# Node-wise programs between the edge passes of a four-layer graph network: six program phases per gap against one block, tile by tile

## The chip, the cores and the metric

The kernel runs on one core of a Trainium2 chip. The time is device microseconds (us) of one execution, median of three runs. TensorE does the matrix products, VectorE, ScalarE and GpSimd the element-wise work, and SyncE issues most DMAs. The profile records one execution.

## What is computed

3,125 nodes with 256 features each, 53,125 edges, all in float32. Four graph layers follow each other, each with a residual and a row norm around it. What lies between two edge passes works node by node:

```python
# end of layer 1 (8 heads)
out = jax.nn.elu(agg).reshape(n_nodes, h * c) + feat @ W_res
x = _layernorm(x + out)
# layer 2; what follows the first line stands in a loop of two, agg is the attention over the edges and the node itself
h = x @ w_in + b_in
xn = _layernorm(h, ln1_g[l], ln1_b[l])
q, k, v = xn @ wq[l] + bq[l], xn @ wk[l] + bk[l], xn @ wv[l] + bv[l]
...
h = h + agg @ wo[l] + bo[l]
xn2 = _layernorm(h, ln2_g[l], ln2_b[l])
h = h + gelu(xn2 @ w1[l] + b1[l]) @ w2[l] + b2[l]          # 256 -> 1024 -> 256
# behind the second of them
x = _layernorm(x + h)
all_h = einsum('ni,rio->nro', x, weight)                    # 8 relations: 256 -> 2048
```

The edge passes of layers 0 to 3, the sorting of the edges ahead of them and the last batch norm are the rest of the program.

## The kernel before

The nodes lie in 25 tiles of 128 (NT = 25), held in SBUF as one tensor `x` of 128 partitions by 25 by 256 (`h` inside layer 2 is the same tensor). The program is a row of phases. Each is a block with one instruction stream for each engine, and a block ends when all its engines are done; the next then allocates its buffers, loads its weights and starts. Three gaps lie between the edge passes. I call them A, B and C:

- A, behind the edge pass of layer 1 (`edge1`): `attend_update` (line 1794: divide by the head sums, ELU, add the residual projection, add to x, norm), `move` (line 2079: x to `x_rows` in HBM), `project` for w_in (line 1540 on), `Affine` (line 1868: statistics of the norm, and h saved to `h_rows`), `project` for q, k, v, whose output goes to `kv_rows`, from which the next edge pass gathers.
- B, behind the first attention pass (`edge2_0`): `self_merge` (line 2030: each node's own score and value merged with the edge sums, v and h loaded again from HBM), `project` for wo, `Affine`, `feed_forward` (line 1914), `Affine`, `project` for q, k, v.
- C, behind the second (`edge2_1`): `self_merge`, `project` for wo, `Affine`, `feed_forward`, `norm_into` (line 1845: x + h, norm), `project` for the 8 relations to `rel_rows`.

Inside `project` and `feed_forward` the work is already pipelined over tiles: ScalarE copies a tile (and applies the norm), TensorE turns it by two transposes (lines 1676, 1979), ScalarE or VectorE moves it out of PSUM, TensorE multiplies (lines 1666, 1990, 1972), VectorE or ScalarE takes the product out, SyncE stores it. `project` keeps 3 PSUM banks for turned tiles and 5 for products. `self_merge`, `attend_update`, `norm_into` and `Norm.statistics` (line 1745) work on whole 128 by 6400 tensors, or over all 25 tiles, on VectorE alone.

Of the kernel before, what the change touches and what calls it, by code (L numbers as in the profile page):

```python
# [1844 lines left out]
def norm_into(nc, tag, x, y, add=None, add_dram=None):  # L1845

    with Phase(nc, tag) as ph:
        norm = Norm(ph)
        own, loaded = ph.sem("own"), ph.sem("loaded")
        block = ph.block()  # L1850

        @block.sync
        def _(sp):
            sp.dma_start(add[:, :, :], node_rows(add_dram)).then_inc(loaded, 16)

        @block.scalar
        def _(act):
            norm.act(nc, act)

        @block.vector  # L1860
        def _(dve):
            step = Chain(dve, own)
            dve.wait_ge(loaded, 16)
            step(nc.vector.tensor_tensor(y[:, :, :], x[:, :, :], add[:, :, :], ALU.add))
            norm.dve(nc, dve, step, y, y)


class Affine:

    def __init__(self, nc, hold, tag, x, gain, bias, loads=()):
        self.scale, self.shift = hold.sb("row_scale", [P, NT]), hold.sb("row_shift", [P, NT])
        self.gain, self.bias = hold.sb("gain", [P, 2]), hold.sb("bias", [P, 2])
        with Phase(nc, tag) as ph:
            norm = Norm(ph)
            own, loaded = ph.sem("own"), ph.sem("loaded")
            block = ph.block()

            @block.sync  # L1880
            def _(sp):
                for dst, a in ((self.gain, gain), (self.bias, bias)):
                    sp.dma_start(dst[:, :], a.rearrange("(c p) -> p c", p=P), allow_slow_non_contiguous=True).then_inc(loaded, 16)
                for dst, a in loads:
                    sp.dma_start(dst, a, allow_slow_non_contiguous=True).then_inc(loaded, 16)
                sp.wait_ge(loaded, 32 + 16 * len(loads))

            @block.scalar
            def _(act):
                norm.act(nc, act)  # L1890

            @block.vector
            def _(dve):
                norm.scale_and_shift(nc, dve, Chain(dve, own), x, self.scale, self.shift)

    def copy(self, nc, out, x, t):

        return nc.scalar.activation(out, flat_tile(x, t), ACT.Identity, bias=self.shift[:, bass.ds(t, 1)],
                                    scale=self.scale[:, bass.ds(t, 1)])


class Dense:


    def __init__(self, ph, w1, b1, w2, b2):
        FF = w1.shape[1]
        self.w1, self.w2 = ph.sb("w1", [P, 2, FF]), ph.sb("w2", [P, FF // P, C])
        self.b1, self.b2 = ph.sb("b1", [P, FF // P]), ph.sb("b2", [P, C])
        self.loads = [(self.w1[:, :, :], w1.rearrange("(c p) f -> p c f", p=P)),
                      (self.w2[:, :, :], w2.rearrange("(f p) c -> p f c", p=P)),  # L1910
                      (self.b1[:, :], b1.rearrange("(f p) -> p f", p=P)), (self.b2[:, :], b2.partition_broadcast(P))]


def feed_forward(nc, k, tag, h, affine, dense):

    w1_s, w2_s, b1_s, b2_s = dense.w1, dense.w2, dense.b1, dense.b2
    FS = 4
    F = w2_s.shape[1]
    with Phase(nc, tag) as ph:
        copy = [ph.sb(f"copy{u}", [P, C]) for u in range(FS)]  # L1920
        turned = [ph.sb(f"turned{u}", [P, 2, P]) for u in range(FS)]
        inner = [ph.sb(f"inner{u}", [P, F, P]) for u in range(FS)]
        turn_p = [ph.ps(f"turn_p{n}", [P, 512]) for n in range(2)]
        up = [ph.ps(f"up{n}", [P, F // 2, P]) for n in range(4)]
        down = [ph.ps(f"down{n}", [P, 512]) for n in range(2)]
        copied, turn, moved, raised, bent, lowered, added, biased = (
            ph.sem(n) for n in ("copied", "turn", "moved", "raised", "bent", "lowered", "added", "biased"))
        block = ph.block()

        def tiles(eng, step):  # L1930

            def body(i):
                for u in range(FS):
                    step(i * FS + u, u)

            rounds(eng, NT // FS, body)
            for t in range(NT // FS * FS, NT):
                step(t, t % FS)

        def there(t):  # L1940
            return not isinstance(t, int) or 0 <= t < NT

        @block.scalar
        def _(act):
            def bend(t, u):
                after(act, lowered, t - FS + 1)
                for f in range(F):
                    act.wait_ge(raised, (2 * t + f // (F // 2) + 1))
                    last = nc.scalar.activation(inner[u][:, f, :], up[2 * (u % 2) + f // (F // 2)][:, f % (F // 2), :],
                                                ACT.Gelu, bias=b1_s[:, f:f + 1])  # L1950
                    if f % (F // 2) == F // 2 - 1:
                        last.then_inc(bent, 1)

            def fetch(t, u):
                after(act, turn, t - FS + 1)
                affine.copy(nc, copy[u][:, :], h, t).then_inc(copied, 1)

            def step(t, u):
                if there(t + 1):
                    fetch(t + 1, (u + 1) % FS)  # L1960
                bend(t, u)

            fetch(0, 0)
            tiles(act, step)

        @block.tensor
        def _(pe):
            def lower(t, u):
                pe.wait_ge(bent, 2 * t + 2)
                after(pe, added, t - 1)  # L1970
                for f in range(F):
                    last = nc.tensor.matmul(down[u % 2][:, 0:C], inner[u][:, f, :], w2_s[:, f, :], start=(f == 0), stop=(f == F - 1))
                last.then_inc(lowered, 1)

            def turn_tile(t, u):
                pe.wait_ge(copied, t + 1)
                after(pe, moved, t - 1)
                for c in range(2):
                    last = nc.tensor.transpose(turn_p[u % 2][:, c * P:(c + 1) * P], copy[u][:, c * P:(c + 1) * P], k.ident[:, :])
                last.then_inc(turn, 1)  # L1980

            def step(t, u):
                if there(t + 1):
                    turn_tile(t + 1, (u + 1) % FS)
                pe.wait_ge(moved, t + 1)
                for half in range(2):
                    after(pe, bent, (t - 2) * 2 + half + 1)
                    for f in range(half * F // 2, (half + 1) * F // 2):
# [12 lines left out]
        def _(dve):  # L2001
# [13 lines left out]
            def step(t, u):  # L2015
# [5 lines left out]
                if there(t - 2):  # L2021
                    add(t - 2, (u - 2) % FS)
# [317 lines left out]
```

## Time and profile before

| | us |
|---|---|
| median of three runs (lowest, highest) | 5543.89 (5540.01, 5545.29) |
| the profiled execution, its own time | 5544.67 |
| its span, first to last instruction | 5542.8 |
| gap A, 2358.3 to 2562.8 | 204.5 |
| gap B, 3262.0 to 3636.8 | 374.8 |
| gap C, 4336.4 to 4846.1 | 509.7 |
| busy over the span: TensorE, VectorE, GpSimd, ScalarE | 3813.8, 3581.9, 2921.2, 1690.4 |

How to read the rows. The view of windows gives for each stretch its length, then busy us and count of TensorE's matmuls, of its weight loads, of VectorE, ScalarE and GpSimd, then the granted TensorE clock as a share of full speed, the busy share of the DMA engines and GB/s. The timeline gives start, length, engine, line, operation, output and input tiles, shapes and count; in brackets stands how long the engine had been idle and what released it (`PEq`: another engine's queue at a block's change). A float32 product counts as two matmul records. The groups by line give busy us, mean ns of one instruction, and idle time just before them. A, B and C were set from the last instruction on `edge` tiles to the first of the next pass.

### The profile page before, as it was taken

How to read it: one execution, taken by the hardware profiler on the slowest of the kernel's cores; microseconds unless marked ns; L12 is line 12 of the kernel's file. 1: busy time of each engine (PE TensorE's matmuls, PEld its weight loads, DVE VectorE, ACT ScalarE, POOL GpSimd, SP SyncE). 2: the span in 40 equal slices, each digit the busy share in tenths (PEclk: the TensorE clock that was granted, in tenths of full speed). 3: DMA queues.
4: the chain of work that ended last, by engine and by line, in shares of the span. 5: the costliest groups of instructions: out<-in, count | busy, mean ns of one | idle time of the engine just before them, and what ended most of it. 6: DMA issues, size and time to landing. Idle time of an engine off the chain costs nothing. (4 is left out here: it accounts for less than half of the span.)

```text
span 5542.8 us, 60231 instructions
## 1 busy us (share of the span) xinstructions
PE 3813.8 (69%) x16239; PEld 2908.4 (52%) x16239; DVE 3581.9 (65%) x6927; ACT 1690.4 (30%) x3460; POOL 2921.2 (53%) x2898
## 2 busy tenths in 40 slices
PE   1666577774896888737777758877777496955551
PEld 0565266662345666625555538655555394444441
DVE  8998755556775777767999963479999612232226
ACT  0001622222782222124555523345555232200000
POOL 3676677776775777503666610056666000077771
PEclk9756776666996777768999979989999798977775
DMA  1243144443103444525777740167777202333333
GB/s 47 53 97 71 39 134 134 132 125 43 30 3 96 133 132 135 91 85 168 209 211 208 208 98 17 57 197 210 209 209 194 76 0 84 145 105 105 105 104 44
DMA packets 280734, 629.96 MB, mean 114 GB/s; under 512 B 70604, under 2 KB 125232, under 8 KB 277296
## 3 DMA queue, kind: packets, MB, share of 16 engines
q0 software_dynamic: 159168, 436.21, 31.0%
q1 hardware_dynamic: 121328, 190.89, 10.6%
q8 instruction: 111, 1.82, 0.1%
q14 instruction: 127, 1.04, 0.1%
HBM read 560.35 MB, written 65.91 MB: 113 GB/s over the span
## 5 line engine op out<-in xcount | busy, mean ns | idle before, releaser
L1001 PE MATMUL edge_sums<-edge_rows,edge_hot 128*128 128x272 f32 (+2 forms) x3712 | 1251.2, 502 | 652.1 <-issue 250.2
L934 POOL DMA_INDIRECT edge_rows<-kv_rows,dst_index x928 | 877.4, 945 | 1102.8 <-POOLq L89 415.0
L1001 PEld LDWEIGHTS edge_sums<-edge_rows,edge_hot 128*128 128x128 f32 x3712 | 917.7, 255 | 917.3 <-issue 543.6
L934 POOL DMA_INDIRECT edge_rows<-rel_rows,dst_other_index x464 | 438.7, 946 | 691.6 <-ACTq L89 550.5
L934 POOL DMA_INDIRECT begun_rows<-xl_rows,dst_index x464 | 450.9, 972 | 199.6 <-issue 131.6
L934 POOL DMA_INDIRECT edge_rows<-rows,src_index x464 | 438.8, 946 | 161.5 <-issue 133.3
L203 POOL DMA_INDIRECT table_src<-src_src_stage_all x333 | 413.5, 1242 | 158.4 <-issue 100.0
L1272 PE MATMUL edge_own_rows<-dst_x,edge_hot_t 128*128 x1856 | 462.0, 394 | 38.8 <-ACT edge_hot_t L965 22.8
L1011 DVE TENSOR_TENSOR l_acc<-l_acc,edge_sums 128x258 f32 (+1 forms) x464 | 198.0, 427 | 366.5 <-PE edge_sums L1001 344.1
L1272 PEld LDWEIGHTS edge_own_rows<-dst_x,edge_hot_t 128*128 128x128 f32 x1856 | 354.2, 196 | 107.7 <-issue 53.9
L1011 DVE TENSOR_TENSOR last_acc<-last_acc,edge_sums 128x256 f32 x232 | 97.7, 421 | 429.6 <-PE edge_sums L1001 429.4
L1666 PE MATMUL proj_prod<-proj_w,proj_turned 128*128 128x512 f32 (+1 forms) x900 | 367.9, 555 | 1.0 <-ACT proj_turned L1614 0.9
L203 POOL DMA_INDIRECT table_dst<-front_dst_stage_all x233 | 297.0, 1275 | 106.8 <-issue 70.1
L982 ACT ACTIVATE edge_hot<-all_ramp,dst_local 128x128 f32<-128x128 f32 x928 | 283.6, 399 | 145.8 <-PE edge_sums L1001 145.8
L1001 PE MATMUL edge_sums<-begun_rows,begun_hot 128*128 128x264 f32 x928 | 310.4, 499 | 2.9 <-DVE begun_rows L1162 2.7
L1078 DVE TENSOR_TENSOR edge_rows<-edge_own_rows,edge_rows 128x1024 f32<-128x1024 f32 x232 | 282.7, 1218 | 41.2 <-DMA edge_rows<-kv_rows,dst_index 41.1
L962 ACT ACTIVATE edge_where<-edge_where,all_neg_row 128x1024 bf16<-128x1024 bf16 x232 | 263.3, 1135 | 72.3 <-DMA edge_where<-local_dst 55.0
L1084 DVE TENSOR_REDUCE edge_score<-edge_rows 128x64 f32<-128x2048 f32 x116 | 265.2, 2286 | 12.1 <-DVE edge_rows L1078 0.9
L1162 DVE TENSOR_TENSOR edge_rows<-edge_rows,edge_turn_p 128x1024 f32<-128x1024 f32 x232 | 271.8, 1213 | 0.7 <-ACT edge_rows L1381 0.7
L965 ACT ACTIVATE edge_hot_t<-edge_where,all_ones 128x1024 f32<-128x1024 bf16 x232 | 266.5, 1149 | 17.8 <-PE edge_own_rows L1272 10.3
L758 PE MATMUL dst_rank_found<-dst_count,dst_rank_low_hot 128*125 (+1 forms) x850 | 194.8, 387 | 102.5 <-DVE dst_rank_low_hot L729 102.5
L1011 DVE TENSOR_TENSOR l2a_acc<-l2a_acc,edge_sums 128x272 f32 x464 | 202.5, 436 | 95.6 <-PE edge_sums L1001 43.5
(436 smaller groups left out, 6548.2 us busy)
## 6 DMA issues: line engine op xcount, KB each, us to landing
edge_where<-local_dst SPq DMA_DIRECT2D x174, 256.0 KB, 3.6
dst_rank_keys<-in_dst SPq DMA_DIRECT2D x85, 312.5 KB, 3.4
rel_rows<-proj_out SPq DMA_DIRECT2D x25, 1024.0 KB, 3.8
edge_where<-local_src SPq DMA_DIRECT2D x58, 256.0 KB, 3.4
edge_rows<-kv_rows,dst_index POOLq DMA_INDIRECT x928, 3.8
kv_rows<-proj_out SPq DMA_DIRECT2D x50, 260.0 KB, 2.0
edge_rows<-rows,src_index POOLq DMA_INDIRECT x464, 2.8
begun_rows<-xl_rows,dst_index POOLq DMA_INDIRECT x464, 2.8
```

The costliest lines, as they stand in the source:

```text
L203: pool.indirect_dma_start(out=self.table[:, :], out_offset=bass.IndirectOffsetOnAxis(ap=self.stage_all[:, at, 0:1], axis=0), in_=self.stag ...
L934: pool.indirect_dma_start(out=self.rows[:, h * U + b, 0:self.width], out_offset=None, in_=self.source[:, :], in_offset=bass.IndirectOffset ...
L962: nc.scalar.activation(where[:, :], where[:, :], ACT.Abs, bias=self.k.neg_row[:, 0:1]).then_inc(self.distant, 1)
L965: nc.scalar.activation(self.hot_t[s % TB][:, :, :].rearrange("p t e -> p (t e)"), where[:, :], ACT.Relu, bias=self.k.ones[:, 0:1], scale=- ...
L982: last = nc.scalar.activation(hot[:, t, :], self.k.ramp[:, :], ACT.Abs, scale=-1.0, bias=self.order.local[:, s * HT + t:s * HT + t + 1])
L1001: last = nc.tensor.matmul(sums[p % len(sums)][:, 0:width], self.hot[s % 2][:, 2 * (p % 4) + i, :], self.half(s)[:, 2 * (p % 4) + i, first: ...
L1011: nc.vector.tensor_tensor(into, into, sums[p % len(sums)][:, 0:width], ALU.add).then_inc(stored, 1)
L1078: nc.vector.tensor_tensor(keys, own_rows[j % 2][:, :, :], keys, ALU.mult).then_inc(multiplied, 1)
L1084: nc.vector.tensor_reduce(score[s // 2 % 2][:, s % 2 * HT:(s % 2 + 1) * HT, :], e.half(s)[:, :, 0:C].rearrange("p t (h d) -> p t h d", h=8 ...
L1162: nc.vector.tensor_tensor(v[:, part, :, 0:32], v[:, part, :, 0:32], coef[:, part, :].unsqueeze(3).to_broadcast([P, HT // 2, 8, 32]), ALU.m ...
L1272: last = nc.tensor.matmul(out, lhs_t, flat_tile(own_src, n), start=True, stop=True)
L1666: last = nc.tensor.matmul(prod[(u * nch + n) % SLOTS][:, 0:m], turned[u][:, c2, :], w[:, c2, c:c + m], start=(c2 == 0), stop=(c2 == 1))
```

## The change

`attend_update` for layer 1, `move`, all `project` calls named above, `Affine`, `feed_forward`, `self_merge` and `norm_into` go. In their place `node_stage` builds one block for each gap: Merge (update in A, own score in B and C), Middle (w_in in A, feed-forward in B and C) and Last (q, k, v in A and B; relations in C). All loops are written out, with no registers. Time is cut into slots, q = 0, 1, ...: at slot q an engine treats tile q in one step, tile q-1 in the next, and so on, so that what one engine makes in a slot another takes up in the next. Every norm goes by groups of 5 tiles. The lags from slot to tile are add_lag = 1 in A and 2 in B and C, c_lag = add_lag + 6, e_lag = c_lag + 8; the last slot is 24 + e_lag, so 40 slots in A and 41 in B and C.

The core of the diff:

```diff
+    OUTS = 5 if qkv else 3
+    ring = 4
+    add_lag = 2 if own_merge else 1
+    c_lag = add_lag + 6
+    e_lag = c_lag + 8
+    last_slot = NT - 1 + e_lag
...
+        turn_c, turn_x, down = ph.ps("turn_c", [P, 512]), ph.ps("turn_x", [P, 512]), ph.ps("down", [P, 512])
+        prod_e = [ph.ps(f"prod_e{n}", [P, 512]) for n in range(2)]
...
         @block.sync
         def _(sp):
...
+            def keep(t):
+                after(sp, added_c, t - 4)
+                sp.wait_ge(copied_c, t + 1)
+                sp.dma_start(c.keep[t * P:(t + 1) * P, :], x[:, t, :]).then_inc(saved[t % 5], 16)
...
+        if own_merge:
+            @block.gpsimd
+            def _(pool):
+                def base(t):
+                    pool.wait_ge(have_x[t // SLOTS], 16)
+                    nc.gpsimd.tensor_tensor(x[:, t, :], x[:, t, :], ba[:, :], ALU.add).then_inc(based, 1)
...
+                def offset(t):
+                    pool.wait_ge(copied_c, t + 1)
+                    ins = nc.gpsimd.tensor_tensor(x[:, t, :], x[:, t, :], bc[:, :], ALU.add)
...
+                    nc.gpsimd.tensor_tensor(x[:, t, :], x[:, t, :], before[:, t % (2 * SLOTS), :], ALU.add).then_inc(biased, 1)
...
         @block.scalar
         def _(act):
...
+            for q in range(last_slot + 1):
+                if group(q - add_lag - SLOTS) is not None:
+                    first.root(nc, act, group(q - add_lag - SLOTS))
+                if group(q - c_lag - 6) is not None:
+                    second.root(nc, act, group(q - c_lag - 6))
+                if own_merge and tile(q - 1) is not None:
+                    move_a(q - 1)
+                if not own_merge and tile(q) is not None:
+                    raise_a(q)
...
+                if tile(q - c_lag + 1) is not None:
+                    fetch_c(q - c_lag + 1)
+                if tile(q - e_lag + 2) is not None:
+                    fetch_e(q - e_lag + 2)
+                if not dense and tile(q - e_lag + 1) is not None:
+                    move_out(q - e_lag + 1)
+                if not dense and tile(q - c_lag + 1) is not None:
+                    move_in(q - c_lag + 1)
+                if dense and tile(q - c_lag) is not None:
+                    bend(q - c_lag, 0)
+                    bend(q - c_lag, 1)
+                if not qkv and tile(q - e_lag) is not None:
+                    leave(q - e_lag, 0)
+                    leave(q - e_lag, 2)
...
+        @block.tensor
+        def _(pe):
...
+            for q in range(last_slot + 1):
+                t, t_a, t_e = tile(q - c_lag), tile(q - 1), tile(q - e_lag)
...
+                if own_merge and t_a is not None:
+                    turn_sum(t_a)
+                if dense and t is not None:
+                    raise_half(t, 0)
+                    raise_half(t, 1)
+                if not dense and t is not None:
+                    multiply_in(t)
+                if tile(q - e_lag + 1) is not None:
+                    turn_out(q - e_lag + 1)
+                if t_e is not None:
+                    for n in range(nch):
+                        multiply_out(t_e, n)
+                if tile(q - c_lag + 1) is not None:
+                    turn_in(q - c_lag + 1)
+                if own_merge and t_a is not None:
+                    multiply_sum(t_a)
+                if dense and t is not None:
+                    lower(t)
...
         @block.vector
         def _(dve):
...
+            for q in range(last_slot + 1):
+                t_1, t_add, t_e = tile(q - c_lag - 1), tile(q - add_lag), tile(q - e_lag)
...
+                if t_1 is not None:
+                    add_in(t_1)
+                if group(q - add_lag - SLOTS) is not None:
+                    first.finish(nc, dve, step, group(q - add_lag - SLOTS))
+                if group(q - c_lag - 6) is not None:
+                    second.finish(nc, dve, step, group(q - c_lag - 6))
+                if t_1 is not None:
+                    dve.wait_ge(added_c, t_1 + 1)
+                    second.statistics(nc, x, t_1)
+                if t_add is not None:
+                    add_own(t_add) if own_merge else add_update(t_add)
+                if tile(q) is not None:
+                    merge_own(q) if own_merge else merge_update(q)
+                if t_add is not None:
+                    dve.wait_ge(added_a, t_add + 1)
+                    first.statistics(nc, x, t_add)
+                if group(q - add_lag - 4) is not None:
+                    first.spread(nc, dve, step, group(q - add_lag - 4))
+                if group(q - c_lag - 5) is not None:
+                    second.spread(nc, dve, step, group(q - c_lag - 5))
+                if dense and tile(q - e_lag + 1) is not None:
+                    move_out(q - e_lag + 1)
+                if t_e is not None and qkv:
+                    leave(t_e, 0)
+                    leave(t_e, 1)
+                    post(t_e)
+                if t_e is not None and not qkv:
+                    leave(t_e, 1)
+                    leave(t_e, 3)
+                if dense and tile(q - c_lag + 1) is not None:
+                    move_in(q - c_lag + 1)
```

What the named steps are. On VectorE: `begin_own` and `begin_update` are the small steps on the head sums ahead of slot 0, followed in A and B by the zeroing of 5 output buffers of 128 by 520; `merge_own` is 3 instructions on 256 columns, `merge_update` 2, `add_own` 1, `add_update` 3, `add_in` 1, each `statistics` 1, `spread` 7 and `finish` 2 on 128 by 5; `leave` takes a product out of PSUM, `post` makes the own score with 2. On ScalarE: `fetch` applies a norm, `root` is the Sqrt of 5 tiles' variances, `raise_a` the Exp of the ELU, `bend` four Gelu instructions. On TensorE: `turn_*` are two transposes; `turn_sum` and `turn_out` share one PSUM bank, `down` is one bank, `prod_e` two. SyncE loads and stores rows and x by tiles or groups of 5, and issues all weight loads of the block ahead of its slots. Edge passes, sorting, layer 0 and the last norm are as before.

## Rows read from the trace of the kernel before

**Rows 1.** Windows over stretches A, B, C: busy us by engine, clock
```profile
2358.30:2562.80 204.50, 103.73 (x400) 68.96 (x400) 140.77 (x329) 57.27 (x129) 0.00 (x0) 0.75 0.26 89
...
3262.00:3636.80 374.80, 286.80 (x1650) 240.09 (x1650) 164.06 (x411) 124.00 (x356) 0.00 (x0) 0.88 0.16 55
...
4336.40:4846.10 509.70, 393.68 (x1850) 277.14 (x1850) 152.72 (x331) 138.72 (x381) 0.00 (x0) 0.88 0.21 80
```

**Rows 2.** Windows, feed-forward and q-k-v projection of B
```profile
3353.80:3540.00 186.20, 183.72 (x1246) 171.77 (x1246) 34.29 (x99) 68.51 (x224) 0.00 (x0) 0.99 0.00 0
...
3566.90:3636.80 69.90, 65.14 (x233) 39.24 (x231) 54.92 (x144) 27.46 (x64) 0.00 (x0) 0.99 0.25 96
```

**Rows 3.** Timeline, VectorE: start, us, line, tiles, idle before
```profile
3283.19 6.83 DVE L2074 TENSOR_TENSOR l2a_agg<-l2a_acc,self_both 128x6400 f32<-128x6400 f32 x1 [15.65 <-DMA dst_x<-h_rows]
...
2434.53 0.42 DVE L1705 TENSOR_TENSOR proj2in_out<-proj2in_prod,proj2in_b 128x256 f32<-128x256 f32 x1 [18.56 <-PE proj2in_prod L1666]
```

**Rows 4.** Timeline, TensorE warm: the transposes that open a tile
```profile
3320.74 0.38 PE L1676 MATMUL proj2o_turn_p<-all_ident,proj2o_copy 128*128 128x128 f32 x2
...
3321.82 0.38 PE L1676 MATMUL proj2o_turn_p<-all_ident,proj2o_copy 128*128 128x128 f32 x2
...
2497.55 0.38 PE L1676 MATMUL proj_turn_p<-all_ident,proj_copy 128*128 128x128 f32 x2
...
2500.35 0.38 PE L1676 MATMUL proj_turn_p<-all_ident,proj_copy 128*128 128x128 f32 x2
...
3369.22 0.38 PE L1979 MATMUL ffn_turn_p<-all_ident,ffn_copy 128*128 128x128 f32 x2
...
3376.47 0.38 PE L1979 MATMUL ffn_turn_p<-all_ident,ffn_copy 128*128 128x128 f32 x2
...
4677.95 0.38 PE L1676 MATMUL proj_turn_p<-all_ident,proj_copy 128*128 128x128 f32 x2
...
4685.04 0.38 PE L1676 MATMUL proj_turn_p<-all_ident,proj_copy 128*128 128x128 f32 x2
```

**Rows 5.** Timeline, TensorE, start of the wo projection
```profile
3308.78 2.07 PE L1666 MATMUL proj2o_prod<-proj2o_w,proj2o_turned 128*128 128x256 f32 x4
```

**Rows 6.** Timeline, VectorE: opening steps, statistics, two dependent steps
```profile
2360.14 6.82 DVE L1832 TENSOR_TENSOR up_hp<-l_acc 128x6400 f32<-128x6400 f32 x1
...
2396.99 8.27 DVE L1749 BATCH_NORM_STATS2 up_stats<-dst_x  x25 [0.35 <-DVE dst_x L1839]
...
2475.85 3.97 DVE L1689 MEMSET proj_out<- 128x776 f32 x5 [1.46 <-PEq L89]
...
2498.54 0.43 DVE L1729 TENSOR_TENSOR proj_tmp<-dst_x,proj_out 128x256 f32<-128x256 f32 x1
...
2499.00 0.42 DVE L1730 TENSOR_REDUCE l2a_self_score<-proj_tmp 128x8 f32<-128x256 f32 x1
...
3266.97 0.57 DVE L2070 TENSOR_TENSOR self_both<-self_both,self_z 128x400 f32<-128x400 f32 x1
```

**Rows 7.** Groups by line, ScalarE, A to C: busy, mean ns
```profile
L1949 ACT ACTIVATE ffn_inner<-ffn_up,l2f_b 128x128 f32<-128x128 f32 x400 | 114.1, 368 | 221.1 <-PE ffn_up L1990 221.1
...
L1898 ACT ACTIVATE ffn_copy<-dst_x,l2f_row_shift,l2f_row_scale 128x256 f32 (+1 forms) x50 | 30.4, 611 | 1.7 <-PEq L89 1.7
...
L1618 ACT ACTIVATE proj2o_turned<-proj2o_turn_p 128x256 f32<-128x256 f32 x50 | 19.1, 383 | 28.1 <-PE proj2o_turn_p L1676 28.1
...
L1781 ACT ACT_TABLE_LOAD x5 | 6.4, 1283 | 22.5 <-PEq L89 22.5
```

**Rows 8.** The page's DMA issues: KB each, us to landing
```profile
kv_rows<-proj_out SPq DMA_DIRECT2D x50, 260.0 KB, 2.0
```

**Rows 9.** Timeline, VectorE, first instruction after A
```profile
2562.83 0.13 DVE L1068 MEMSET edge_link<- 8x34 f32 x2 [4.43 <-PEq L98]
```

**Rows 10.** Groups by line, GpSimd, whole span
```profile
L371 POOL MEMSET src_bucket_empty<- 128x232 int32 x1 | 0.5, 508 | 0.1
```

**Rows 11.** Windows, 100 us inside the last edge pass
```profile
4900.00:5000.00 100.00, 57.94 (x162) 44.52 (x161) 28.18 (x50) 0.00 (x0) 75.62 (x81) 0.74 0.37 105
```

More of the change, by code:

```diff
@@ L1842, in _, with __init__ @@
             norm.dve(nc, dve, step, x, x)
-def norm_into(nc, tag, x, y, add=None, add_dram=None):
-    with Phase(nc, tag) as ph:
-        norm = Norm(ph)
-        own, loaded = ph.sem("own"), ph.sem("loaded")
+class Merge:
+    def __init__(self, kind, acc, rows, **more):
+        self.kind, self.acc, self.rows = kind, acc, rows
+        self.self_score, self.h_dram, self.w, self.b = (more.get(n) for n in ("self_score", "h_dram", "w", "b"))
+        self.guard = more.get("guard")
+class Middle:
+    def __init__(self, kind, w, b, **more):
+        self.kind, self.w, self.b = kind, w, b
+        self.w2, self.b2, self.gain, self.bias, self.keep = (more.get(n) for n in ("w2", "b2", "gain", "bias", "keep"))
@@ new lines, in bend, with move_a @@
+            def bend(t, half):
+                act.wait_ge(raised, 2 * t + half + 1)
+                after(act, lowered, t - 1)
+                for f in range(half * H, (half + 1) * H):
+                    ins = nc.scalar.activation(inner[t % 2][:, f, :], up[half][:, f % H, :], ACT.Gelu, bias=b1[:, f:f + 1])
+                ins.then_inc(bent, 1)
+            def move_a(t):
+                act.wait_ge(turned_1, t + 1)
+                after(act, multiplied_a, t - ring + 1)
+                nc.scalar.activation(turned_a[t % ring][:, :, :].rearrange("p c n -> p (c n)"), turn_x[:, 0:C],
+                                     ACT.Copy).then_inc(moved_a, 1)
@@ L1862, in _ @@
             step = Chain(dve, own)
[L1863 to L1899, printed above, removed]
@@ L1902 @@
[L1902 to L1911, printed above, removed]
@@ L2079, in move @@
[L2079 to L2089 removed]
+            if own_merge:
+                sums = a.acc[:, :, 0:VW].rearrange("p t (h e) -> p t h e", e=33)
+                peak = a.acc[:, :, VW:VW + 8]
+            else:
+                every = a.acc[:, :, :].rearrange("p t (h e) -> p t h e", e=33)
@@ new lines, in post @@
+            def post(t):
+                dve.wait_ge(left_v, nch * t + 1)
+                step(nc.vector.tensor_tensor(tmp[:, :], x[:, t, :], out[t % OUTS][:, 0:C], ALU.mult))
+                nc.vector.tensor_reduce(e.self_score[:, t, :], tmp[:, :].rearrange("p (h d) -> p h d", h=8), AX.X,
+                                        ALU.add).then_inc(posted, 1)
+            begin_own() if own_merge else begin_update()
+            if qkv:
+                for n in range(OUTS):
+                    nc.vector.memset(out[n][:, :], 0.0).then_inc(padded, 1)
+                dve.wait_ge(padded, OUTS)
```

587 lines of the change are left out of this document (394 added, 193 removed).

## The prediction

> **What bounds the kernel now.** I read the page first, then the timeline at each change of phase, then windows over the parts between two edge passes. TensorE is busy 69% of the span and VectorE 65%, but these are means over stages with different limits, and the edge passes are not touched. What the change can move are the stretches A, B and C, 204.5 + 374.8 + 509.7 = 1089.0 us, and in them GpSimd does nothing and TensorE is busy 103.7, 286.8 and 393.7 us [rows 1]. Inside a phase that multiplies, TensorE sets the pace: it is busy 183.7 of 186.2 us in the feed-forward of B and 65.1 of 69.9 us in its q-k-v projection, at a granted clock of 0.99 [rows 2]. So the time to be had lies between those phases: whole-tensor steps on VectorE (6.82 us each, 8.27 us for 25 statistics), weights and rows that are loaded only when a phase begins, and the filling of a pipeline at each phase: VectorE sat idle 15.65 us for the reload of h and 18.56 us until the first product of w_in [rows 3, 6]. Over B TensorE idles 374.8 - 286.8 = 88 us, over C 116 us, over A 101 us.
>
> **TensorE's work a tile** does not change. The start of one tile's transposes to the next one's is 1.08 us for wo (and for w_in, the same shape), 2.80 us for q-k-v, 7.25 us for the feed-forward, 7.09 us for the relations, all at full clock [rows 4]. The second feed-forward figure comes from tiles 2 and 3, which the kernel of before has written out without registers, so written-out code alone costs nothing there. A slot with all three stages then costs TensorE 1.08 + 7.25 + 2.80 = 11.13 us in B, 1.08 + 7.25 + 7.09 = 15.42 us in C, and 1.08 + 2.80 = 3.88 us in A.
>
> **VectorE's work a tile.** A 256-column step that the next one must wait for takes 0.46 us from start to start, one that nobody waits for about 0.33, as do the statistics (8.27 / 25) [rows 6]. In A: merge_update 0.7, add_update 1.4, two statistics 0.7, add_in 0.5, leave and post 2.1, so 5.4 us, and the small steps on 5 tiles' variances, 9 for each norm and group at some 0.2 us, 4 us every 5 slots, so 0.8: 6.2 us a slot. This is more than TensorE's 3.88, so A becomes VectorE's. In B the sum is 1.4 for merge_own, 0.5 + 0.5 for the additions, 0.7 statistics, 1.4 for moving turned tiles in and out, 2.1 leave and post, 0.8: 7.4 us beside 11.13. The order inside a slot counts too. VectorE's slot can open only when TensorE's `lower` of the slot before is done, since add_in comes first, and `move_in`, which TensorE's next slot needs, comes last. Between them it waits for turn_out (4.2 us into TensorE's slot) and for two products: 4.2 + 0.7, products until 5.9, leave to 7.3, post to 8.2, move_in to 8.9 us, up to 10.3 in a slot with a spread. That is under 11.13 with 0.8 us left; in C, 12.3 us under 15.42. So B and C stay TensorE's.
>
> **The sum, gap by gap.**
> A. Opening steps 1.8 us (start of the first whole-tensor step less 2358.3) and the zeroing, 3.97 x 520 / 776 = 2.7 [rows 6]. Slots 0 to 7, merge, add and statistics, 2.5 and some 0.3 of waiting for the Exp: 8 x 2.8 = 22. Slots 8 to 14 with add_in and the norms: 7 x 4.0 = 28. Slots 15 to 24: 6.2 and 0.2 of hand-over, 64. Slots 25 to 31, with no merging left, go round a loop of TensorE and ScalarE (multiply_in 0.9, turn_out 0.2, multiply_out 2.6, turn_in 0.4, moving out of PSUM 0.38 and hand-overs [rows 7]): 7 x 4.9 = 34. Slots 32 to 39: 8 x 3.0 = 24. End 4.4, as now [rows 9]. To this come the table loads. ScalarE now changes from Exp to Sqrt and back for each of ten groups, and a load is 1.28 us [rows 7]; finish waits for it at the head of VectorE's slot. The load needs no input and can run before the variances are there, so of 10 x 1.28 I take 8 us, bounds 0 and 10 x 2 x 1.28 = 26. A: 189 us.
> B. Opening to the end of its last small step, 3266.97 + 0.57 - 3262.0 = 5.6 [rows 6], zeroing 2.7. Slots 0 to 7: TensorE is little busy and the clock low. A product that takes 1.03 warm took 2.07 us there [rows 5], so the loop turn_sum 0.6, ScalarE 0.38, multiply_sum 1.9, hand-overs 0.3 gives 3.2 us: 26. The first group's norm, once, 3. Slots 8 to 15: 8.33 and a wait of 0.4, because only turn_in and multiply_sum (1.08) stand between the second half of `up` and `lower`, while four Gelus take 4 x 0.37 = 1.5 [rows 7]: 8 x 8.73 = 70, and 3 for Gelu and Sqrt tables in two of them. Slots 16 to 25: 10 x 11.13 = 111.3. Slots 26 to 32: 7 x 10.05 = 70.4. Slots 33 to 40, VectorE: 8 x 3.1 = 25. End 4.4. B: 321 us.
> C. 5.6 + 26 + 3 + 70 + 3, then 10 x 15.42 = 154.2, 7 x (7.25 + 7.09) = 100.4, 8 x 7.09 = 56.7, end 6 (the last store is four times as wide as those of 2.0 us [rows 8]). C: 425 us.
> Together 935 against 1089, so 154 us less: 15 from A, 53 from B, 85 from C. Against the profiled execution's own 5544.67 (span 5542.8 and 1.9 around it) that is 5391, and the median of the runs lies 0.8 below that execution: 5390 us.
>
> **What is costed at nothing, and its cover.** All weight loads are issued ahead of the slots and are needed in slot 7 and slot 15, 20 us and more after the start; without that cover one costs about what the entry of w_in shows, up to 18 us [rows 3]. Rows and x by groups of 5: the first must land before slot 0, hidden by 8 us of opening steps. `keep` in A: SyncE is in order, so it stands behind store(q - e_lag), which waits for `post` at the end of VectorE's slot; add_in needs it two slots later, 12 us against a landing of 2.0 [rows 8]. ScalarE in B: 4 + 4 Gelus 3.0, two norm copies 1.2, a move 0.4: 4.6 of 11.13, so its 20 table loads (26 us) fit.
>
> GpSimd's additions (`base`, `offset`, one more in C) have no row. The nearest is a fill of 232 columns in 0.51 us [rows 10], against 5.5 us of room for each in B; I take them as hidden, bounds 0.5 and 5.5. The Trainium skill (SBUF — State Buffer, the section on SBUF's two separate sides) says that a VectorE operation with two SBUF inputs and a GpSimd operation that reads SBUF take one port pair as an exclusive lock, so these additions would hold up VectorE's merging and statistics; no trace of this kernel shows the two together. By that rule the slot of B is at risk where its room is 0.8 us, and it is the last rival below that it would feed.
>
> **Rivals.** (1) Hand-overs set the slots. Each engine waits for others four to eight times a slot, and many waits sit inside a slot, not a slot apart: turn_sum, move_a, multiply_sum; up, Gelu, lower; turn_out, move_out. For it: VectorE has only 0.8 us of room in B's worst slots, and A's loop goes through three engines. Against it: feed_forward has the same hand-overs and holds TensorE at 0.99 [rows 2]. At 0.75 us more in each of 122 slots: +92, 5482 us. (2) The clock. In A TensorE has work for about 60% of a slot. In the last edge pass it is busy 58% at a mean clock of 0.74 [rows 11]. Were it at 1.2 GHz throughout A, its 3.88 becomes 7.8 and bounds the slots from 15 on: 10 x 1.4 + 7 x 2.9 + 8 x 2.6 = 55, so 5445 us. The Trainium skill (TensorE: Matmul & The Clock Gate, Part 1) has a gate that follows how busy the engine has been, which would make the lean slots cold; the trace agrees in that the first tiles of wo ran at half speed [rows 5], and in B and C the lean slots are already priced cold. (3) Slower than before: GpSimd becomes the bound. It has 2 additions a slot in B and 3 in C, in order, so from 11.13 / 2 = 5.6 and 15.42 / 3 = 5.1 us each on it sets the slot. The gain of 154 is gone where 25 x (2p - 11.13) + 25 x (3p - 15.42) reaches 154, at p = 6.5 us; at p = 8 the time is 5390 + 336 = 5726 us. The nearest row, 0.51 us, is far from it.
>
> **How the numbers follow.** Forecast 5390 with 0.77, hand-overs 0.12, clock 0.08, GpSimd 0.02, and 0.01 for an end within 0.2%. The forecast's own bounds: below, no table stalls (-8), VectorE's steps overlapping their waits in A (-10), fills of 2.5 us instead of 3.2 (-11), no Gelu wait (-12): 5349. Above, 26 instead of 8 for tables and 0.3 us more in 122 slots: 5445. Of the hand-over case the range takes in the near part: 5345 to 5455. Faster by more than 0.2% (11 us, about what can be told from no change here) 0.96, within 0.01, slower 0.03.
>
> **What would show it.** B should have slots of 11.1 us with TensorE without gaps and clock near 1, C slots of 15.4, A slots of about 6.3 with VectorE nearly full; stretches of 189, 321 and 425 us, the edge passes unchanged. Wrong would be: TensorE waiting for VectorE's move_in or ScalarE's Gelu in B; a granted clock under 0.8 in A with TensorE full; VectorE instructions longer than 0.43 us beside GpSimd's; or edge passes that lengthen, since their buffers move in SBUF.

## The result: 3.2% faster, and the profile after

The changed kernel takes 5364.68 us (median, 5354.85 to 5372.13); the kernel before, run beside it, 5544.59 (5540.01 to 5549.89). The ratio is 0.9676, 95% interval 0.9664 to 0.9688. The forecast was 5390, range 5345 to 5455; the range held the time, which came out 25 us below the forecast.

The profiled execution took 5366.55 us. Its page, first the busy times, then the granted clock in 40 slices:

```profile
span 5364.4 us, 58815 instructions
...
PE 3834.8 (71%) x16239; PEld 2913.6 (54%) x16239; DVE 3601.9 (67%) x7185; ACT 1719.9 (32%) x3429; POOL 3033.3 (57%) x3023
...
PEclk9755866666897777769899999989999899977775
```

Windows over A, B and C after, then the edge passes behind A, B and C (the columns of [rows 1]):

```profile
2360.40:2544.40 184.00, 117.86 (x400) 71.28 (x400) 135.45 (x424) 83.63 (x175) 0.00 (x0) 0.85 0.29 99
3242.30:3551.90 309.60, 287.38 (x1650) 237.73 (x1650) 184.36 (x507) 118.01 (x305) 42.24 (x50) 0.97 0.20 67
4252.70:4665.90 413.20, 393.15 (x1850) 275.89 (x1850) 158.99 (x400) 147.86 (x355) 60.54 (x75) 0.98 0.27 100
2544.40:3242.30 697.90, 523.68 (x2117) 397.68 (x2117) 614.80 (x1017) 363.89 (x813) 440.04 (x464) 0.93 0.71 200
3551.90:4252.70 700.80, 526.29 (x2117) 399.38 (x2117) 614.57 (x1017) 363.97 (x813) 440.24 (x464) 0.92 0.72 199
4665.90:5364.40 698.50, 342.72 (x932) 262.19 (x932) 246.56 (x364) 0.64 (x2) 440.06 (x464) 0.69 0.36 92
```

Against [rows 1], A went from 204.5 to 184.0 us (forecast 189), B from 374.8 to 309.6 (321), C from 509.7 to 413.2 (425): 182 us less in the three. The edge passes stayed within some 2 us each. TensorE's work in B and C is what it was (286.8 and 287.4, 393.7 and 393.2 us); its idle time fell from 88 to 22 us in B and from 116 to 20 in C.

One full slot of B on TensorE (start, us, line, operation, out<-in, shapes):

```profile
3420.78 0.38 PE L2182 MATMUL nodes_turn_x<-all_ident,nodes_agg 128*128 128x128 f32 x2
3420.99 3.74 PE L2215 MATMUL nodes_up<-nodes_turned_c,nodes_w 128*128 128x128 f32 x32
3424.57 0.38 PE L2182 MATMUL nodes_turn_x<-all_ident,nodes_copy_e 128*128 128x128 f32 x2
3424.79 2.75 PE L2243 MATMUL nodes_prod_e<-nodes_we,nodes_turned_e 128*128 128x512 f32 x8
3427.37 0.38 PE L2182 MATMUL nodes_turn_c<-all_ident,nodes_copy_c 128*128 128x128 f32 x2
3427.59 1.03 PE L2207 MATMUL nodes_prod_a<-nodes_wa,nodes_turned_a 128*128 128x256 f32 x4
3428.45 3.62 PE L2223 MATMUL nodes_down<-nodes_w,nodes_inner 128*128 128x256 f32 x16
3431.91 0.38 PE L2182 MATMUL nodes_turn_x<-all_ident,nodes_agg 128*128 128x128 f32 x2
```

From one turn_sum to the next are 3431.91 - 3420.78 = 11.13 us, and no line shows TensorE waiting. The same slot on VectorE:

```profile
3420.98 0.42 DVE L2344 TENSOR_TENSOR dst_x<-dst_x,nodes_down 128x256 f32<-128x256 f32 x1 [2.69 <-PE nodes_down L2223]
...
3422.43 0.95 DVE L2309 TENSOR_TENSOR nodes_rows<-nodes_rows,nodes_both 128x256 f32<-128x256 f32 x1
...
3424.99 0.73 DVE L2354 TENSOR_SCALAR nodes_turned_e<-nodes_turn_x,nodes_gain_e,nodes_bias_e 128x128 f32<-128x128 f32 x2
...
3426.71 0.42 DVE L2369 SCALAR_TENSOR_TENSOR dst_x<-nodes_prod_e,nodes_be 128x256 f32<-128x256 f32 x1 [0.99 <-PE nodes_prod_e L2243]
...
3428.70 0.72 DVE L2336 TENSOR_SCALAR nodes_turned_c<-nodes_turn_c,nodes_gain_c,nodes_bias_c 128x128 f32<-128x128 f32 x2
3432.11 0.42 DVE L2344 TENSOR_TENSOR dst_x<-dst_x,nodes_down 128x256 f32<-128x256 f32 x1 [2.69 <-PE nodes_down L2223]
```

It goes in the order that the forecast told: add_in first, then merging, the second norm's small steps, move_out, the product, post, and last move_in (L2336), done at 3429.42. TensorE's next `up` follows at 3432.12. So VectorE has 2.7 us of room, and that in a slot with a spread. In A it is TensorE that waits for VectorE, once in every slot, and the wait is part of a loop through both engines. TensorE's waits between 2425 and 2515, then TensorE and VectorE around one turn of the loop:

```profile
engine line waited for: us in total, times, longest us
PE nodes_down L2230 <- DVE dst_x L2347: 22.8, 16, 1.6
```

```profile
2494.20 1.10 PE L2230 MATMUL nodes_down<-nodes_wc,nodes_turned_c 128*128 128x256 f32 x4 [1.51 <-DVE dst_x L2347]
...
2495.36 2.75 PE L2243 MATMUL nodes_prod_e<-nodes_we,nodes_turned_e 128*128 128x512 f32 x8
...
2499.83 0.45 PE L2230 MATMUL nodes_down<-nodes_wc,nodes_turned_c 128*128 128x256 f32 x1 [1.51 <-DVE dst_x L2347]
```

```profile
2497.28 0.42 DVE L2369 SCALAR_TENSOR_TENSOR dst_x<-nodes_prod_e,nodes_be 128x256 f32<-128x256 f32 x1 [2.59 <-PE nodes_prod_e L2243]
...
2499.27 0.41 DVE L2347 TENSOR_TENSOR dst_x<-nodes_down,nodes_bc 128x256 f32<-128x256 f32 x1
```

multiply_in (L2230) writes the one bank `down` and may not start before add_in (L2347) has read it. add_in opens VectorE's next slot, behind leave and post, and these wait for multiply_out (L2243). 2499.83 - 2494.20 = 5.63 us a turn, and that is the slot of A from 16 to 31, but for one of 5.68 and three of 5.75.

### The profile page after: what moved, and what is told of

The parts are those of the page before. It is cut to its first block and busy times, and to the rows that moved or that the text cites. A ratio compares the mean times of both kernels' runs of the same rounds, so it can differ in the third digit from the quotient of the medians.

```text
span 5364.4 us, 58815 instructions
## 1 busy us (share of the span) xinstructions
PE 3834.8 (71%) x16239; PEld 2913.6 (54%) x16239; DVE 3601.9 (67%) x7185; ACT 1719.9 (32%) x3429; POOL 3033.3 (57%) x3023
## 5 line engine op out<-in xcount | busy, mean ns | idle before, releaser
L1011 DVE TENSOR_TENSOR l_acc<-l_acc,edge_sums 128x272 f32 (+2 forms) x928 | 400.7, 432 | 470.0 <-PE edge_sums L1001 399.2
L2243 PE MATMUL nodes_prod_e<-nodes_we,nodes_turned_e 128*128 128x512 f32 (+1 forms) x800 | 315.4, 542 | 1.1 <-DVE nodes_out L2370 0.9
L2074 POOL TENSOR_TENSOR dst_x<-dst_x,nodes_bc 128x256 f32<-128x256 f32 x50 | 41.7, 835 | 453.6 <-ACT nodes_copy_c L1911 453.6
```

What stands on the lines that cost most here:

```text
L1011: nc.vector.tensor_tensor(into, into, sums[p % len(sums)][:, 0:width], ALU.add).then_inc(stored, 1)
L2243: ins = nc.tensor.matmul(prod_e[n % 2][:, 0:m], turned_e[t % ring][:, h, :], we[:, h, at:at + m], start=(h == 0), stop=(h == 1))
```

## The experiments

All runs below were made where the edge passes take longer, for a reason that the runs don't show. Windows over two of them, in the first run of the changed kernel below:

```profile
2884.00:3800.50 916.50, 593.05 (x2117) 448.54 (x2117) 616.39 (x1017) 363.76 (x813) 438.61 (x464) 0.77 0.55 152
4109.90:5027.30 917.40, 592.51 (x2117) 448.12 (x2117) 616.04 (x1018) 363.78 (x813) 438.64 (x464) 0.77 0.55 152
```

They move 152 GB/s where the first chip moved 200, and take 917 us instead of 698 to 701. A, B and C are alike on all the chips, so each run is read by these three stretches.

### The changed kernel as it stands, twice

The first time, with the next three runs:

> The changed kernel again, on the chip of the runs beside it, so that they can be compared with it. All theories: within 0.3% of its first median of 5364.7 us, gaps of 184, 310 and 413 us.

6218.27 us beside 6388.41 for the kernel before, ratio 0.9747 (0.9728 to 0.9766); the two medians alone give 0.9734, and in the runs below too their quotient differs a little from the recorded ratio, always inside its interval. A, B and C took 183.7, 309.4 and 414.8 us. The second time, with the last three:

> The changed kernel again, as the reference for the runs beside it. Both theories: the three stretches between the edge passes stay at 184, 309.4 and 414.8 us, and the ratio to the kernel before lies at 0.975, as in the first run of it on this kind of chip, whose edge passes take longer.

6126.21 beside 6299.54, ratio 0.9723 (0.9708 to 0.9738), stretches 184.4, 309.2 and 415.5 us. The gain in microseconds, 170 and 173, is that of the first chip (180) less some 7 to 10. This difference does not lie in the three stretches, which are 181 and 180 us shorter than in [rows 1]; where it lies, these runs don't show. The ratio is nearer to 1 mainly because the part that is not touched is longer.

### Gap A alone

The block for A as in the changed kernel; B and C with the programs of before.

> Gap A by the new block, gaps B and C with the phases of before. Theory 1, the gaps do not touch each other: gap A 184 us, B 375, C 510, so 20 us less than before, about 5525. Theory 2, part of the gain of B and C comes from elsewhere (buffers, an edge pass that runs otherwise): the edge passes or gap B differ from before by more than 3 us.

6367.2 us, ratio 0.9974 (0.9962 to 0.9985), 21 us less. Windows over A, B and C:

```profile
2699.30:2883.20 183.90, 118.38 (x400) 71.72 (x400) 135.44 (x423) 83.63 (x175) 0.00 (x0) 0.84 0.29 99
3795.70:4171.60 375.90, 287.36 (x1650) 239.96 (x1650) 164.14 (x411) 124.22 (x356) 0.00 (x0) 0.88 0.16 55
5091.00:5601.00 510.00, 392.64 (x1850) 276.60 (x1850) 152.30 (x330) 138.96 (x381) 0.00 (x0) 0.89 0.22 80
```

A has all of its gain and B and C are those of [rows 1] within about 1 us. The stretches don't affect each other, and the gain is a sum, as the forecast had it.

### The block without the overlap of its parts

```diff
-    c_lag = add_lag + 6
-    e_lag = c_lag + 8
+    c_lag = add_lag + 27
+    e_lag = c_lag + 29
```

Merging, feed-forward and projection now come one after another inside the block; everything else (tiles, groups of 5, no whole-tensor steps, weights loaded ahead) stays.

> The same three blocks, but the lags are 27 and 29 slots instead of 6 and 8, so that merge, middle and last part of a gap run one behind another over all 25 tiles. Theory 1, what pays is that the lean stages lie beside the full ones: gap B becomes 8 + 28 x 2.5 + 25 x 7.7 + 25 x 2.9 + 6 = 349 us (310 now), C 451 (413), A 227 (184), about 120 us more, 5485. Theory 2, what pays is that block entries, late loads and whole-tensor steps are gone: at most 30 us more than now, about 5395.

6384.53 us, ratio to the kernel before 0.9997 (0.9987 to 1.0007): with the parts apart nothing is left of the gain. A, B and C took 213.0, 381.5 and 485.8 us. Windows over B, then over 23 tiles of its feed-forward part alone, and TensorE's waits in 165 us of that:

```profile
3833.80:4215.30 381.50, 314.23 (x1650) 248.11 (x1650) 177.87 (x506) 109.63 (x297) 38.17 (x50) 0.93 0.16 54
...
3928.60:4124.60 196.00, 172.72 (x1153) 157.78 (x1152) 40.17 (x129) 74.25 (x218) 15.95 (x22) 1.00 0.04 14
```

```profile
PE nodes_down L2223 <- ACT nodes_inner L2113: 19.2, 19, 1.0
```

B was expected at 349 and C at 451 us. Of the 32 and 35 us that they took more, 20 each are one thing: with nothing between `up` and `lower` but turn_in, TensorE waits 1.0 us a tile for the Gelus of the second half, so a feed-forward tile takes 8.52 us where the expectation had 7.7. (The rest lies in the merging part, some 8 us, and in the last.) The old program, at 186.2 us for 25 tiles [rows 2], took 7.45 a tile; against it the block loses 25 x 1.07 = 27 us in each of B and C. (A was expected at 227 us and took less, its slots being 1.83 us in the middle part and 2.90 in the last.) So the block with its parts apart is no better than the old programs: A and B take 8.5 and 6.7 us more than before, C 24 less, which happens to come out even. So the overlap is worth 381.5 - 309.4 = 72 us in B, 71 in C and 29 in A, 172 in all, and some 54 of these by covering those Gelus. Part of the rest is the clock: the same products keep TensorE busy 314.2 us in B instead of 287.4 and 418.3 in C instead of 395.2, and the merging part alone has a granted clock of 0.73. There a slot whose product takes 1.13 us is some 1.83 us long, one whose product takes 2.06 some 2.97:

```profile
3833.80:3930.00 96.20, 61.19 (x217) 42.10 (x218) 71.02 (x191) 17.14 (x44) 22.23 (x28) 0.73 0.36 110
```

This does not show that the other half of the change (no entries between phases, no late loads, no whole-tensor steps) is worth nothing. The three stretches of this run are 1080.3 us against 1089.0 before, and 54 of the 1080.3 are the Gelu wait that the old feed-forward does not have. Without it, an estimate from these numbers, the parts one after another would take some 1026 us, 63 less than before. No run tests that.

### VectorE's room in B

Twelve idle additions of 256 columns on VectorE ahead of move_in in every slot of B.

```diff
                 if dense and tile(q - c_lag + 1) is not None:
+                    if qkv:
+                        for n in range(12):
+                            nc.vector.tensor_tensor(idle[:, n, :], bc[:, :], bc[:, :], ALU.add)
                     move_in(q - c_lag + 1)
```

> Twelve idle additions of 256 columns stand ahead of move_in on VectorE in each slot of B; at 0.34 us from start to start they are 4.1 us. Theory (the order inside the slot counts: add_in comes after TensorE's lower, move_in last, and TensorE's next slot needs move_in): in a full slot move_in is now done 2.7 us before it is needed, so the full slots grow from 11.13 by 4.1 - 2.7 = 1.4 to 12.5 us, and TensorE waits for move_in. Rival (only the sum of VectorE's work counts): VectorE works some 7.4 to 7.9 us of 11.13, 3.2 us and more are free, so with 4.1 us more the slot grows by 0.9 at most, to 12.0, and no wait for move_in shows but one for a full VectorE. Where both say more than 11.13, the wait of TensorE tells them apart: its length for move_in, and whether VectorE has idle time in the slot.

One run, 6169.5 us. B took 356.8 instead of 309.2 us. The full slots are 12.60 us: 1.47 more for 4.11 us of additions (one group of twelve), so the room was 2.64, close to the 2.7 of the timeline. TensorE's waits over nine full slots; then windows over `up` in a later slot, and over one full slot of 12.6 us:

```profile
PE nodes_up L2216 <- DVE nodes_turned_c L2337: 11.1, 9, 1.4
```

```profile
4001.20:4006.60 5.40, 5.34 (x33) 5.34 (x34) 1.56 (x10) 1.15 (x4) 0.00 (x0) 0.69 0.02 3
3886.10:3898.70 12.60, 11.39 (x66) 9.48 (x66) 10.00 (x32) 5.23 (x13) 1.41 (x3) 1.00 0.07 24
```

The wait is for move_in, and VectorE has 2.6 us idle in that slot. So the order inside the slot decides, not the sum of VectorE's work; by the rival the slot would have been 12.0 us at most. The later slots, 26 to 32, had a surprise: with one product less they should be no longer, and four of seven are 14.1 to 14.3 us. TensorE now waits 2.3 us there, and `up` after such a wait takes 5.42 us instead of 3.74: granted clock 0.69, so part of it ran at 1.2 GHz. VectorE's next steps wait for this slow `up`, so the whole slot grows by its 1.7 us. The waits of 1.2 us in the full slots had no such effect (clock 1.00).

### GpSimd's load and the shared port

Two idle additions of 512 columns behind each of GpSimd's additions in B and C.

```diff
+    def more():
+        pool.wait_ge(idled, sent[0])
+        sent[0] += 2
+        for n in range(2):
+            nc.gpsimd.tensor_tensor(idle_c[:, n, :], idle_a[:, :], idle_b[:, :], ALU.add).then_inc(idled, 1)
```

> GpSimd does two idle additions of 512 columns behind each of its additions in B and C, which takes nothing away from the other engines but the port. Between one addition of 256 columns at some 0.85 us and twice that for 512 columns, GpSimd then works 2 x 0.85 + 4 x 1.6 = 8.1 us of a full slot of B (11.13) and 12.2 of 15.4 in C, so it is no bound itself. Theory A (the port is locked for a whole GpSimd instruction): each VectorE step with two SBUF inputs, three in merge_own and one in post, waits up to 1.6 us, so it takes up to 2.0 us where it now takes 0.95 at most; up to 5 us a slot ahead of move_in, which has 2.7 us of room: full slots of B 12 to 13.4 us. Theory B (the two engines only alternate on the port): the VectorE steps stay at 0.95 us at most, more of them at that, 4 x 0.53 = 2.1 us a slot, inside the room: slots stay at 11.13. Theory C (no lock, GpSimd matters only as a bound): VectorE's steps are 0.42 or what they are now, slots 11.13 and 15.4.

One run, 6173.0 us, with B at 326.7 and C at 434.2. First the price in the changed kernel itself (first chip): L2309, the product of the rows and their weight, in a slot of the filling where GpSimd rests; the same line and L2310 in the full slots (duration ns min/median/max); GpSimd's additions by line:

```profile
3262.29 0.42 DVE L2309 TENSOR_TENSOR nodes_rows<-nodes_rows,nodes_both 128x256 f32<-128x256 f32 x1
```

```profile
L2309 DVE TENSOR_TENSOR nodes_rows<-nodes_rows,nodes_both x8: 411/949/953, 3355.8 to 3434.2; 128x256 f32<-128x256 f32 x8
...
L2310 DVE TENSOR_TENSOR nodes_agg<-nodes_agg,nodes_rows x8: 424/628/836, 3356.8 to 3434.7; 128x256 f32<-128x256 f32 x8
```

```profile
L2070 POOL TENSOR_TENSOR dst_x<-dst_x,nodes_ba 128x256 f32<-128x256 f32 x25 | 22.0, 893 | 47.5 <-DMA nodes_ba<-in_L_gnn_bo 47.5
L2074 POOL TENSOR_TENSOR dst_x<-dst_x,nodes_bc 128x256 f32<-128x256 f32 x25 | 20.9, 835 | 207.5 <-ACT nodes_copy_c L1911 207.5
```

With the load, the same step as L2310 in full slots; two stretches of GpSimd's timeline in the filling, beside VectorE's merging and at its end; and two of VectorE's small steps there:

```profile
L2325 DVE TENSOR_TENSOR nodes_agg<-nodes_agg,nodes_rows x8: 1376/1378/1381, 3867.6 to 3946.7; 128x256 f32<-128x256 f32 x8
```

```profile
3768.10 0.91 POOL L2079 TENSOR_TENSOR dst_x<-dst_x,nodes_ba 128x256 f32<-128x256 f32 x1
3768.97 2.85 POOL L2075 TENSOR_TENSOR nodes_idle_c<-nodes_idle_a,nodes_idle_b 128x512 f32<-128x512 f32 x2
...
3782.81 0.72 POOL L2079 TENSOR_TENSOR dst_x<-dst_x,nodes_ba 128x256 f32<-128x256 f32 x1
3783.50 2.48 POOL L2075 TENSOR_TENSOR nodes_idle_c<-nodes_idle_a,nodes_idle_b 128x512 f32<-128x512 f32 x2
```

```profile
3783.60 1.19 DVE L1892 TENSOR_SCALAR nodes_first_mean<-nodes_first_mean 128x5 f32<-128x5 f32 x1
...
3784.77 1.23 DVE L1894 TENSOR_SCALAR nodes_first_var<-nodes_first_var 128x5 f32<-128x5 f32 x1
```

A VectorE step with two SBUF inputs takes 0.42 us alone, 0.95 beside GpSimd's additions of 256 columns and 1.38 beside those of 512. So its wait grows with the length of GpSimd's instruction (0.53, then 0.96 us) and is not one fixed share. It ends with the GpSimd addition that was running when the step began: the L2309 of the full slot above starts at 3422.43, inside an addition that ends at 3423.10, and ends itself at 3423.38. That is theory A for the single step, at 1.38 us where it allowed up to 2.0. Its forecast for the slots failed: they were to grow to 12 us or more, and none of B's is over 11.40. Additions that take one input from PSUM keep their time beside the load (add_own 0.40 in the filling), and so do the statistics (0.41). Steps with a single input are not all spared: the two TENSOR_SCALAR shown take 0.17 and 0.16 us without the load. GpSimd pays too: 0.91 instead of 0.72 for 256 columns.

What it costs the kernel is small in the full slots: in B six of ten grew by 0.16 to 0.27 us and four stayed at 11.13; in C three of ten went from 15.42 to 16.4. Most of B's 17.5 us more (326.7 against 309.2) comes from the filling, where the first add_in is at 54.6 us instead of 39.0: there GpSimd's chain of 3.68 us a tile takes the place of TensorE's and VectorE's 1.83. That is the mechanism of the third rival, a bound by GpSimd, in the one phase whose slots are short; at the true price of 0.9 us an addition it is far off.

### Two banks for `down`, and the zeroing moved

The loop of A broken open: two PSUM banks, so that multiply_in waits only for the add_in of the tile before the last.

```diff
-                after(pe, added_c, t)
+                after(pe, added_c, t - 1)
                 for h in range(2):
-                    ins = nc.tensor.matmul(down[:, 0:C], turned_c...
+                    ins = nc.tensor.matmul(down[t % 2][:, 0:C], turned_c...
```

> Two banks for `down` in gap A instead of one, nothing else. Theory 1, gap A is set by a loop through that bank: TensorE's multiply_in waits for VectorE's add_in of the tile before, add_in stands behind leave and post of the slot before, and these wait for multiply_out. With two banks the slots 15 to 24 fall from 5.63 us to about 5.2 (VectorE's own work) and slots 25 to 31 from 5.63 to 4.2 to 4.9; the gap loses 8 to 14 us, about 5354 us. Theory 2, VectorE's own work sets 5.63: no change, gap 184 us.

A took 177.0 instead of 183.7 us, 6.6 less where 8 to 14 were expected; the median was 6207.41 (0.9724, 0.9702 to 0.9745), whose interval overlaps that of the changed kernel, so the stretch shows the gain and the whole time does not. TensorE no longer waits for add_in; between 2764 and 2815 this is its longest wait:

```profile
PE nodes_down L2232 <- ACT nodes_turned_c L2132: 6.9, 8, 1.0
```

In slots 25 to 31 the mean is 4.62 us, as expected from TensorE's and ScalarE's loop; they give 7.0 us, and slot 15 gives 2.6 more (6.7 instead of 9.3). Slots 16 to 24 lose 3.2 again: seven stayed at 5.6 to 5.8, and two were 7.2; in the first of these TensorE, after waits of 1.2 and 1.0 us, took 1.98 us for the multiply_in that is 1.10 in the loop above, so its clock had fallen (0.83 over those 10 us). So in slots 16 to 24 the bank was only one of two bounds that happened to agree. VectorE is the other: between 2798 and 2804 in this run it goes from one instruction to the next without idle time. With the second change, the output buffers zeroed by GpSimd (the lines for B; A gets a GpSimd part that does only this):

```diff
-                for n in range(OUTS):
-                    nc.vector.memset(out[n][:, :], 0.0).then_inc(padded, 1)
...
+                if qkv:
+                    for n in range(OUTS):
+                        nc.gpsimd.memset(out[n][:, :], 0.0).then_inc(padded, 1)
```

> Two PSUM banks for `down` in A, as in the run with two banks (A took 177.1 instead of 183.7 us), and the zeroing of the output buffers on GpSimd instead of VectorE in A and B. Theory: the zeroing stands in VectorE's queue ahead of the first slot and costs its 2.7 us there, in A and in B, so A takes 174.4 and B 306.7 us, 12 us less than the changed kernel in all. Rival: the first slot waits anyway (in A for the rows, in B for the Exp of the opening steps), GpSimd's zeroing holds VectorE's merging up by the shared port, and only the 6.6 us of the banks are left.

6113.04 us (6105.79 to 6121.44) beside 6126.21 (6120.61 to 6132.38) for the changed kernel: 13.2 us less; their ratios to the kernel before, 0.9706 (0.9693 to 0.9720) and 0.9723 (0.9708 to 0.9738), overlap a little, so by the whole time alone it would be weak. The stretches are plain. A and B in this run, and the zeroing:

```profile
2665.90:2840.80 174.90, 118.63 (x400) 71.25 (x400) 133.00 (x418) 83.85 (x175) 2.54 (x5) 0.83 0.31 104
3731.90:4038.00 306.10, 287.06 (x1650) 237.84 (x1650) 178.73 (x501) 118.28 (x305) 43.77 (x55) 0.98 0.21 68
```

```profile
2665.82 2.62 POOL L2071 MEMSET nodes_out<- 128x520 f32 x5 [37.51 <-POOLq L89]
```

A has 9.4 us less (6.6 of the banks, 2.8 of the zeroing), B 3.0, and C, with neither edit, its 415.5. It is the best version here.

## Why the prediction was right, by its steps

**The pace of the full slots** was exact: 11.13 us in B, 15.41 to 15.42 in C, 10.05 and 14.33 behind them, and 8.74 to 8.75 in slots 9 to 13, where 1.08 + 7.25 = 8.33 leaves 0.4 for the Gelu wait. These 24 slots (9 to 32) carry 243 us of B's 309.6 and 316 of C's 413.2, and they hold what the forecast was surest of: TensorE is the bound and warm.

**The sum by phases** (the limits are starts of add_in, which the first time opens slot 9 in B and C and slot 8 in A; the forecast's terms are put together to the same limits):

```
            B: forecast  measured    C: forecast  measured
to slot 8       46.0       39.4         43.3       36.1
slots 9-15      64.1       61.4         64.1       61.4
slots 16-25    111.3      111.3        154.2      154.2
slots 26-32     70.4       70.1        100.4      100.1
end             29.4       27.4         62.7       61.5
            A: forecast  measured
slots 0-7       26.5       27.0
slots 8-14      28         29.0
slots 15-24     64         60.4
slots 25-31     34         39.4
end             28.4       28.2
table loads      8         in the rows above
```

**The filling was mis-sized.** The step "slots 0 to 7: 3.2 us each" took a cold product of 2.07 us for all of them. In B three of the first eight ran so: the first two (2.07 and 1.99 us) and one behind the wait for the first norm (1.92). The others took 1.13 or less, and the slots between are 1.82 to 1.87 us. TensorE had been busy 4.19 of the 5.8 us before the clock rose. This gives most of the 7 us in each of B and C. The first norm group did cost its 3 us or so (slots of 3.80 and 3.38). **The tables for Gelu and Sqrt in slots 9 to 15**, 3 us in B and C, cost 0.1 to 0.2: the load lies ahead of a wait. Both misses have the same sign in both gaps: 19 of the 28 us by which the three stretches came out shorter than forecast (907 against 935).

**VectorE's room in B** was put at 0.8 us in the worst slot, and is 2.7 there. The spread's small steps took 0.9 us in all, where the forecast had 1.4, and lie in the time until turn_out, in which VectorE would have waited. The mechanism (move_in last, and what TensorE's next slot waits for once the room is used up) was confirmed by the padded run.

**A came out near (184.0 against 189) partly by luck, with two errors of opposite sign in it.** Slots 15 to 24 took 3.6 us less than forecast, slots 25 to 31 took 5.4 more. VectorE's slot is 5.63 and not 6.4 us (steps that don't depend on one another start 0.33 apart), and the loop from slot 25 on is not TensorE with ScalarE at 4.9 us but the single bank at 5.63. The forecast saw the chain through ScalarE and missed that add_in stands behind post in VectorE's order. The run with two banks showed the forecast loop, at 4.62. Table loads were about right in size: in all of A VectorE's waits for the Sqrt, load and Sqrt together, come to 8.1 us, against 8.

**What was costed at nothing stayed hidden, but for one load**: no wait for a weight or for `keep` shows in the slots from 9 on, and GpSimd's additions, bounded by 0.5 and 5.5 us, are 0.72 to 1.02. In C, which has no zeroing in front, TensorE's first transposes start at 4261.01, when the bias of wo has landed, though VectorE's first merged tile is done at 4259.66: 1.35 us later. The rule that was cited beside the additions from the Trainium skill (SBUF — State Buffer, the section on SBUF's two separate sides) holds here, with 0.42 us against 0.95, but its wait lies in the room of B's slot. The forecast read it as holding up the statistics too; they stay at 0.41 to 0.43. It also named a VectorE instruction of more than 0.43 us beside GpSimd's as a sign of being wrong: such came, and cost the full slots nothing.

**The rivals.** Hand-overs (1) set nothing in the full slots of B and C. In A they do, since the loop through the bank is one of hand-overs, at 1.5 us of waiting a turn; and where a part is left alone, as in the run with the parts apart, they cost 1.07 us a tile. The cold clock (2) held in A only up to the first q-k-v product, as these windows show, the first over slots 8 to 14:

```profile
2387.40:2416.40 29.00, 17.63 (x44) 9.82 (x42) 22.83 (x76) 15.05 (x29) 0.00 (x0) 0.56 0.23 77
...
2425.00:2477.00 52.00, 37.96 (x144) 23.54 (x144) 46.39 (x149) 33.18 (x69) 0.00 (x0) 1.00 0.27 95
```

That product took 4.24 us and its slot 9.3. After it the clock stayed at 1.00 with TensorE busy 73%, more than the 58% of the edge pass at 0.74 [rows 11]. The two slots of 7.20 us in the run with two banks show that this rival was not far. GpSimd as the bound (3) appears only with the added load.

## What to carry to other kernels

Let parts with different bounds run side by side, tile by tile, and put another part's work between two steps that hand over to each other inside a slot: here the overlap was worth 172 us, a third of it by covering the Gelus, and without it the same block only equalled the old programs. Work out each engine's order inside a slot, not only its sum, and for every single buffer write down the loop writer, reader, whatever stands ahead of the reader in its queue, and back: that loop was the one wrong bound here. In the filling, price the clock tile by tile and not as cold throughout.

## What the runs showed of the hardware that was not expected

- VectorE steps with two SBUF inputs wait until the running GpSimd addition ends: 0.42 us alone, 0.95 beside 256 columns, 1.38 beside 512; GpSimd's own 0.72 becomes 0.91. A TENSOR_SCALAR of 5 columns with one SBUF input took up to 1.24 us instead of 0.17 beside the 512-column additions, while additions with a PSUM input and the statistics kept their time.
- TensorE kept its full clock in slots where it was busy 73%, and in slots of 12.6 us with a wait of 1.2; it lost it in slots with one wait of 2.3 us (`up` then took 5.42 instead of 3.74 us), and once in A after waits of 1.2 and 1.0 us.
- The edge passes ran at 152 GB/s on one chip and at 200 on another, 917 against 700 us (on a third at 156 to 157, in 886 and 894 us), while A, B and C differed by 2.3 us at most.
